# One-hot rows for the slot list of a mixture of experts: on ScalarE instead of VectorE

## Chip, cores and metric

The kernel runs on one core of one Trainium2 chip. Its time is the device time of one execution in microseconds (us); lower is better. The core's engines each run their own list of instructions and meet at semaphores: TensorE (PE in the profile), VectorE (DVE), ScalarE (ACT), GpSimd (POOL) and SyncE (SP), whose list issues most of the DMAs.

## What is computed

Input is `x` of 4 x 1024 tokens with 256 features, all in float32. After a layer norm without weights the result is `x + mamba(xn) + moe(xn)`.

```
mamba:  rn = rmsnorm(xn) * norm_w;  skip = rn @ skip_w.T;  x = silu(conv4(rn @ in_w.T) + conv_b)
        delta = softplus(x @ wd1.T @ wd2.T + wd2_b);  Bm = x @ wB.T;  Cm = x @ wC.T
        h[t] = exp(delta[t] * A) * h[t-1] + delta[t] * x[t] * Bm[t]      (512 channels x 16 states)
        out = xn + ((h . Cm) + x * W_D) * silu(skip) @ out_w.T
moe:    gates = softmax(xn @ Wr)                                          (8 experts)
        inds = the 2 experts with the smallest gates; scores = their gates, normed to sum 1
        out[t] = sum over the 2: score * (silu(xn @ W1[e]) * (xn @ V1[e])) @ W2[e]
```

The mixture is computed sparsely: each token has two (token, expert) pairs, 8192 in all, which are sorted by expert into at most 71 tiles of 128 slots. For that the kernel needs a slot list: for each slot its token and its score.

## The kernel before

**The scan and its units.** The tokens are cut into 16 chunks of 256. A chunk is 32 units: half of the 512 channels (two tiles of 128 partitions) times one of the 16 states. For each unit ScalarE makes `exp(delta * A)` (`exps`, L554, two activations), VectorE makes the product with B (`products`, L1138) and the recurrence (`scan`, L1159, two instructions), GpSimd multiplies two units at once by C (`parts`, L763), and PE adds the result up in PSUM (`sum_parts`, L858) with transposes by the identity. Buffers limit how far the engines can be apart: ScalarE's exps are two units ahead of VectorE in program order, and exps of unit w wait for the scan of unit w - 4. GpSimd is two units behind, PE four.

**The rest of the work** is cut into pieces, and each has a place: behind which unit of its chunk it stands. `pieces(c)` lists them from tables written out by hand (B_PLACES, O_PLACES, F_PLACES), `places_of(engine)` moves some kinds some units later on one engine (table LATER), and every engine runs, unit after unit, its own part of each piece (`do`). Pieces with B or CV, CW, X2, SP, DL prepare the next chunk: chunk input (B1), projection and copy of it to `xin` (B2, ScalarE's L603), convolution (CV, CW, which in chunks 0 and 2 VectorE does from L1283 on, and otherwise ScalarE and GpSimd), Silu (X2, L617), projections to delta, B and C (B3, B4, SP). O pieces finish the chunk before: Silu of the skip branch (O2, L658) and the output products (O1, O3). The kernel has one queue per engine and no other order.

**The router and the slot list.** In chunk 0, R pieces write the normed rows and their logits, and at unit 30 VectorE has run the last router step (`router_slots`), which leaves for each of the 64 columns of pairs `tile` (which slot tile), `lane` (which of 128 rows), `score` and `back`. STAT_END on the semaphore `stat` marks its end; `steps`, a row of 0 to 127 on all partitions, follows it (`ones_set` 2). In chunk 1, eight M pieces (rounds r of 8 columns) stand behind units 2, 4, 6, 8, 12, 18, 21 and 23. In one round VectorE compares `tiles` with `tile` (L1268, 128 x 568) and `steps` with `lane` (L1271, 128 x 1024, one-hot rows into the buffer `hot[r % 2]`), GpSimd multiplies the first result by `back` (L803) and by `score` (L805), and PE, four units later, adds eight matmuls `hot x vals` to bank X (L1004). `placed` counts PE's rounds: from round 2 on VectorE waits for `placed` r - 1 before it writes the buffers again. `hot_set` tells PE that the one-hot rows are there, `val_set` does for the values. Piece MF behind unit 27 reads bank X on VectorE (L1319, L1321, L1323) into `meta` and `idx`; with `idx_set` SP starts the load of W2, which overwrites these buffers, and GpSimd the first two gathers of tokens (L771). From chunk 2 on the expert tiles run as FA, FB and FC pieces, 71 of them up to chunk 14.

ScalarE takes no part in the M pieces: its `do` has no branch for them. Around them its order is, behind unit 33 Silu of O2 (L658), 35 the y copy (L571) and chunk input (L580, L586), 36 the second Silu, 37 the first xin copy (L603), 40 the second, 51 X2 (L617), 54 B3 (L624, L626), 56 B4 (L638, L640) and 59 SP (L647, L650). Unit 32 is the first of chunk 1. All these names of buffers, `hot`, `vals`, `lane`, `steps`, lie in the space of W2, so the profile calls them `w`.

Of the kernel before, what the change touches and what calls it, by code (L numbers as in the profile page):

```python
# [18 lines left out]
ALU = mybir.AluOpType  # L19
ACT = mybir.ActivationFunctionType  # L20
# [199 lines left out]
def mamba_moe(nc, x, norm_w, skip_wT, in_wT, conv_w, conv_b, wd1T, wd2T, wd2_b, wBCT, A_log, W_D, out_wT,  # L220
# [3 lines left out]
    with ctx:  # L224
# [3 lines left out]
        def sem(name):  # L228
            return ctx.enter_context(nc.semaphore(name))
# [126 lines left out]
        res_out = [sem("res_out0"), sem("res_out1")]  # L356
        id_set = sem("id_set")
        added = sem("added")
        hot_set = sem("hot_set")
        val_set = sem("val_set")  # L360
        placed = sem("placed")
# [170 lines left out]
        def _(act):  # L532
# [40 lines left out]
            def do(piece):  # L573
# [31 lines left out]
                elif kind == "CV" and piece[2] not in DVE_CONV:  # L605
                    e, c = piece[1], piece[2]
                    act.wait_ge(conv, KE * c + e)
                    wait_taken(act, "G" if e < 2 else "V", ("B2", e // 2, c))
                    at_least(act, brow_w, 32 * c)
                    nc.scalar.activation(tap[:, 0, :], xin[:, e, 0:CH], ACT.Identity, bias=cb[:, e:e + 1], scale=cw[:, e, 0:1])  # L610
                    for w in range(1, TAPS):
                        ins = nc.scalar.activation(tap[:, w, :], xin[:, e, w:w + CH], ACT.Copy, scale=cw[:, e, w:w + 1])  # L612
                    ins.then_inc(cva, 1)
                elif kind == "X2":
                    c = piece[2]
                    act.wait_ge(conv, KE * (c + 1))
                    nc.scalar.activation(x2[:, c % 2, :, :], x2[:, c % 2, :, :], ACT.Silu).then_inc(x2r, 1)  # L617
                elif kind == "B3":
                    c = piece[2]
                    wait_full(act, "G", piece)  # L620
                    at_least(act, brow_w, 32 * c)
                    if c >= 1:
                        wait_full(act, "V", ("B4", 1, c - 1))
                    nc.scalar.activation(dtT[:, :], bank["G"][:, 0:CH], ACT.Copy)  # L624
                    act.wait_ge(conv, KE * (c + 1))
                    nc.scalar.activation(brow, bank["G"][0:2 * N, CH:2 * CH], ACT.Copy).then_inc(free["G"], 1)  # L626
                elif kind == "B4":
                    q, c = piece[1], piece[2]
                    b = "HV"[q]
                    if c >= 1:  # L630
                        at_least(act, dlt, c)
                    if c >= 2:
                        wait_full(act, "V", ("O3", 1, c - 2))
                        act.wait_ge(uu, 2 * (c - 1))
                    wait_full(act, b, piece)
                    for i in range(2):
                        e = 2 * q + i
                        nc.scalar.activation(y1[:, e, :], bank[b][:, i * CH:(i + 1) * CH], ACT.Abs,  # L638
                                             bias=db[:, e:e + 1]).then_inc(spx, 1)
                        ins = nc.scalar.activation(delta[:, c % 2, e, :], bank[b][:, i * CH:(i + 1) * CH], ACT.Relu,  # L640
                                                   bias=db[:, e:e + 1])
                    ins.then_inc(free[b], 1)
                elif kind == "SP":
                    step, c = piece[1], piece[2]
                    if step == 0:
                        act.wait_ge(spx, 6 * c + 4)
                        nc.scalar.activation(y1[:, :, :], y1[:, :, :], ACT.Exp, scale=-1.0).then_inc(spx, 1)  # L647
                    else:
                        act.wait_ge(spx, 6 * c + 5)
                        nc.scalar.activation(y1[:, :, :], y1[:, :, :], ACT.Ln, bias=1.0).then_inc(spx, 1)  # L650
                elif kind == "O2":
                    q, c = piece[1], piece[2]
                    b = "GV"[q]
                    wait_full(act, b, piece)
                    if c >= 1:
                        wait_full(act, "V", ("O3", 1, c - 1))
                    act.wait_ge(dlt, min(c + 2, CHUNKS))
                    nc.scalar.activation(y1[:, 2 * q:2 * q + 2, :], bank[b][:, :].rearrange("p (k t) -> p k t", k=2),  # L658
                                         ACT.Silu).then_inc(free[b], 1)
                elif kind == "O3":  # L660
                    s, c = piece[1], piece[2]
                    b = "HV"[s]
                    t = SUB * c + s
                    if c < CHUNKS - 1:
                        wait_full(act, b, piece)
                        if c > 0:
                            wait_landed(act, ("O3", 1, c - 1))
                        nc.scalar.activation(mst[:, s, :], bank[b][:, 0:D], ACT.Copy).then_inc(free[b], 1)
                elif kind == "R":
                    i = piece[1]  # L670
                    if i < TT // 2:
                        if i >= 2:
                            wait_full(act, "V", ("R", i - 1))
                            act.wait_ge(xt_out[i % 2], 16 * (i // 2))
                        for t in (2 * i, 2 * i + 1):
                            nc.scalar.activation(tok[:, t % 4, :], xall[:, t, :], ACT.Identity, bias=nmr[:, t:t + 1],
                                                 scale=rstd[:, t:t + 1]).then_inc(xn_r, 1)
                    if 1 <= i <= TT // 2:
                        for k, t in enumerate((2 * i - 2, 2 * i - 1)):
                            wait_full(act, "HV"[k], piece)  # L680
                            at_least(act, lgt, t - 1)
                            nc.scalar.activation(xT[:, k, :, :], bank["HV"[k]][:, 0:D].rearrange("p (k t) -> p k t", k=KD),
                                                 ACT.Copy).then_inc(free["HV"[k]], 1)
                elif kind == "RA":
                    act.wait_ge(stat, STAT_LOGITS)
                    nc.scalar.activation(rt[:, 1], rt[:, 0], ACT.Exp).then_inc(sact, 1)
                elif kind == "FA":
                    j = piece[1]
                    if j < JT:
                        wait_full(act, "H", piece)  # L690
                        if j > 0:
                            wait_taken(act, "V", ("FB", j - 1))
                        nc.scalar.activation(th, bank["H"][:, :], ACT.Tanh, scale=0.5).then_inc(s_th, 1)  # L693
                    if j > 0:
                        wait_full(act, "G", piece)
                        if j > 1:
                            wait_full(act, "X", ("FC", j - 1))
                        nc.scalar.activation(gT, bank["G"][:, :], ACT.Copy).then_inc(free["G"], 1)
                elif kind == "FB":
                    j = piece[1]  # L700
                    if j + 1 < JT:
                        wait_full(act, "X", piece)
                        nc.scalar.activation(xT[:, (j + 1) % 2, :, :], bank["X"][:, 0:D].rearrange("p (k t) -> p k t", k=KD),  # L703
                                             ACT.Copy).then_inc(free["X"], 1)
                elif kind == "FC" and piece[1] > 0:
                    j = piece[1] - 1
                    wait_full(act, "X", piece)
                    if j == 0:
                        act.wait_ge(idx_set, 2)
                        wait_rows(act)  # L710
                    if j >= 2:
                        wait_landed(act, ("FC", j - 1))
                    nc.scalar.activation(tok[:, 2 + j % 2, :], bank["X"][:, 0:D], ACT.Identity,  # L713
                                         scale=meta[:, j:j + 1]).then_inc(free["X"], 1)
# [356 lines left out]
        def _(dve):  # L1071
# [189 lines left out]
            def value_rows(r):  # L1261
# [4 lines left out]
                tiles = csts[:, TT * EXPERTS + TT:TT * EXPERTS + TT + JT].unsqueeze(1).to_broadcast([P, ROUND, JT])  # L1266
                at_least(dve, val_set, 3 * r)
                v.tensor_tensor(vals[r % 2][:, :, JT:2 * JT], tiles, tile[:, at].unsqueeze(2).to_broadcast([P, ROUND, JT]), ALU.is_equal).then_inc(val_set, 1)  # L1268
                if r == 0:
                    dve.wait_ge(ones_set, 2)  # L1270
                v.tensor_tensor(hot[r % 2], steps.unsqueeze(1).to_broadcast([P, ROUND, P]),  # L1271
                                lane[:, at].unsqueeze(2).to_broadcast([P, ROUND, P]), ALU.is_equal).then_inc(hot_set, 1)

            def do(piece):
                kind = piece[0]
# [125 lines left out]
```

## Time and profile before

| | |
|---|---|
| median of 3 runs | 1282.13 us (1279.8 to 1283.07) |
| the profiled execution: its own time | 1284.09 us |
| its span, from the first to the last instruction | 1282.3 us |
| busy: PE, VectorE, ScalarE, GpSimd | 1073.0, 1170.8, 1013.4, 1003.4 us |
| mean granted TensorE clock | 0.926 |
| DMA | 195.08 MB, mean 152 GB/s |

A line of the timeline has the start, the duration, the engine, the line of the kernel, the operation, output and inputs with their shapes (partitions x elements), and in brackets the idle time before it with what ended it. A line merged from several instructions (x2) has their duration from the first start to the last end. The groups of a view by line have the number of instructions, busy us, mean ns of one, and the idle time of the engine before them. Ends of consecutive instructions of VectorE and ScalarE overlap the next start by some tenths of a microsecond.

### The profile page before, as it was taken

The numbers are of one execution on the slowest core, as the hardware profiler recorded it, in microseconds if no ns is written. First come the engines' busy times: TensorE is split into PE (matmuls) and PEld (weight loads), VectorE is DVE, ScalarE is ACT, GpSimd is POOL, SyncE is SP. The second block draws the span as 40 slices with busy tenths as digits, with TensorE's granted clock in tenths as the row PEclk, the third lists the DMA queues.
The fourth block names the chain that finished last, engine by engine and source line by source line (L and its number), as shares of the span: only waits on it lengthen the run. The fifth ranks groups of instructions, "written<-read, shape, count | busy, mean of one in ns | idle before, by whom it ended". The sixth has DMA issues, their size and how long they took to land.

```text
span 1282.3 us, 20051 instructions
## 1 busy us (share of the span) xinstructions
PE 1073.0 (84%) x5406; PEld 807.0 (63%) x5406; DVE 1170.8 (91%) x2145; ACT 1013.4 (79%) x2153; POOL 1003.4 (78%) x602
## 2 busy tenths in 40 slices
PE   3379376587998989999989999898999999998766
PEld 2268265465766666676767666676767667675555
DVE  5874899899999999999989899999989899999896
ACT  2797345589898888879888898889888898988862
POOL 1396277678898979888888988989898988989654
PEclk8686597799999999899999999999999999999987
DMA  7467723745554453545545454555545455545436
GB/s 227 143 205 253 267 77 106 231 139 146 147 146 140 141 160 120 150 141 145 146 133 155 121 154 138 146 157 144 146 123 155 135 145 148 155 122 140 126 125 190
DMA packets 87117, 195.08 MB, mean 152 GB/s; under 512 B 11184, under 2 KB 47152, under 8 KB 86928
## 3 DMA queue, kind: packets, MB, share of 16 engines
q1 hardware_dynamic: 69008, 171.18, 41.4%
q0 software_dynamic: 17712, 22.55, 10.6%
q8 instruction: 47, 0.77, 0.2%
q14 instruction: 62, 0.51, 0.1%
q10 hardware_dynamic: 288, 0.07, 0.0%
HBM read 171.22 MB, written 26.48 MB: 154 GB/s over the span
## 4 chain that ended last, share of the span: by engine, by line
PE 32%; ACT 21%; POOL 17%; issue 13%; DVE 12%; DMA 4%; DVEq 0%; POOLq 0%; ACTq 0%
POOL part L763 11%; ACT aexp L554 8%; PE yps L858 7%; PE bankX L1051 5%; DVE hb L1159 5%; PE bankV L1041 4%; PE bankH L1017 4%; DVE bps L1138 4%; DMA acc<-scr,idx 3%; ACT tap L612 3%; ACT L554 2%; PE bankG L898 1%; POOL scr L771 1%; POOL acc L819 1%; POOL tap L793 1%
## 5 line engine op out<-in xcount | busy, mean ns | idle before, releaser
L763 POOL TENSOR_TENSOR part<-hb,bcr 128x1024 f32<-128x1024 f32 x256 | 625.2, 2449 | 147.1 <-DVE hb L1159 102.5
L1159 DVE TENSOR_TENSOR_SCAN hb<-aexp,carry,bps 128x256 f32<-128x256 f32 x768 | 545.6, 733 | 11.4 <-ACT aexp L554 11.4
L554 ACT ACTIVATE aexp<-delta,Am 128x256 f32<-128x256 f32 x1024 | 446.9, 503 | 54.2 <-DVE hb L1159 52.7
L858 PE MATMUL yps<-idn,part 128*128 128x128 f32 x2048 | 300.2, 287 | 92.8 <-POOL part L763 88.4
L858 PEld LDWEIGHTS yps<-idn,part 128*128 128x128 f32 x2048 | 250.9, 148 | 164.9 <-POOL part L763 97.7
L1138 DVE TENSOR_TENSOR bps<-ups,bcr 128x512 f32<-128x512 f32 x512 | 345.2, 674 | 1.1
L1159 DVE TENSOR_TENSOR_SCAN hb<-aexp,bps 128x256 f32<-128x256 f32 x256 | 167.8, 673 | 23.9 <-ACT aexp L554 23.3
L1051 PE MATMUL bankX<-w,scr 128*128 x568 | 143.2, 397 | 21.8 <-ACT scr L703 19.4
L1017 PE MATMUL bankH<-w,scr 128*128 x284 | 137.9, 608 | 2.1 <-issue 2.1
L1041 PE MATMUL bankV<-v,scr 128*128 x284 | 134.2, 595 | 4.7 <-ACT xin L603 3.3
L1051 PEld LDWEIGHTS bankX<-w,scr 128*128 128x128 f32 x568 | 107.8, 198 | 43.0 <-issue 29.8
L819 POOL DMA_INDIRECT acc<-scr,idx x71 | 114.2, 1609 | 22.4 <-ACT scr L713 7.9
L793 POOL TENSOR_TENSOR tap<-tap 128x512 f32<-128x512 f32 x56 | 78.4, 1400 | 10.3 <-ACT tap L612 10.0
L771 POOL DMA_INDIRECT scr<-xt,idx x71 | 72.3, 1018 | 12.4 <-issue 7.4
L1017 PEld LDWEIGHTS bankH<-w,scr 128*128 128x128 f32 x284 | 51.0, 195 | 42.6 <-issue 40.6
L1041 PEld LDWEIGHTS bankV<-v,scr 128*128 128x128 f32 x284 | 48.4, 190 | 40.3 <-issue 40.3
L612 ACT ACTIVATE tap<-xin,cw 128x256 f32<-128x256 f32 x168 | 72.5, 496 | 0.0
L713 ACT ACTIVATE scr<-bankX,meta 128x256 f32<-128x256 f32 x71 | 33.1, 466 | 49.1 <-PE bankX L1051 49.1
L1327 DVE SCALAR_TENSOR_TENSOR scr<-scr,bankH 128x512 f32<-128x512 f32 x71 | 47.5, 669 | 26.3 <-ACT scr L693 26.2
L693 ACT ACTIVATE scr<-bankH 128x512 f32<-128x512 f32 x71 | 41.9, 590 | 27.8 <-PE bankH L1017 27.8
L554 ACT ACT_TABLE_LOAD x48 | 61.6, 1283 | 0.9
L424 POOL TENSOR_TENSOR delta<-delta,y 128x1024 f32<-128x1024 f32 x15 | 35.3, 2355 | 33.3 <-ACT y L650 33.2
(187 smaller groups left out, 1616.9 us busy)
## 6 DMA issues: line engine op xcount, KB each, us to landing
bcr<-brows SPq DMA_DIRECT2D x256, 512.0 KB
w<-in_W SPq DMA_DIRECT2D x2, 4096.0 KB, 21.9
xch<-in_x SPq DMA_DIRECT2D x16, 256.0 KB, 3.8
w<-in_x SPq DMA_DIRECT2D x4, 1024.0 KB, 9.8
xt<-scr SPq DMA_DIRECT2D x16, 256.0 KB, 2.8
acc<-scr SPq DMA_DIRECT2D x16, 256.0 KB, 2.7
v<-in_V SPq DMA_DIRECT2D x1, 4096.0 KB, 14.9
acc<-mst POOLq DMA_DIRECT2D x15, 256.0 KB
```

What stands on the lines that cost most here:

```text
L554: nc.scalar.activation(aexp[:, w % EXP_SLOTS, i, :], delta[:, c % 2, e, :], ACT.Exp, scale=Am[:, e, n:n + 1]).then_inc(s_a, 1)
L612: ins = nc.scalar.activation(tap[:, w, :], xin[:, e, w:w + CH], ACT.Copy, scale=cw[:, e, w:w + 1])
L763: nc.gpsimd.tensor_tensor(part[:, slot:slot + 2, :, :], hb[:, state:state + 2, :, :], bcr[:, row:row + 2, CH:2 * CH].unsqueeze(2).to_broad ...
L771: nc.gpsimd.indirect_dma_start(out=tok[:, j % 2, :], out_offset=None, in_=xt, in_offset=bass.IndirectOffsetOnAxis(ap=idx[:, j:j + 1], axis ...
L793: nc.gpsimd.tensor_tensor(tap[:, 0:2, :], tap[:, 0:2, :], tap[:, 2:4, :], ALU.add).then_inc(cvs, 1)
L819: nc.gpsimd.indirect_dma_start(out=acc, out_offset=bass.IndirectOffsetOnAxis(ap=idx[:, j:j + 1], axis=0), in_=tok[:, 2 + j % 2, :], in_off ...
L858: mm = pe.matmul(yps[:, s, i * P:(i + 1) * P], part[:, w % (2 * PART_PAIRS), i, s * P:(s + 1) * P], idn[:, :], start=(n == 0 and s == 0 an ...
L1017: mm = pe.matmul(bank["H"][:, :], xT[:, j % 2, k, :], w1[:, bass.ds(col + k * FF, FF)], start=(k == 0), stop=(k == KD - 1))
L1041: mm = pe.matmul(bank["V"][:, :], xT[:, j % 2, k, :], v1[:, bass.ds(columns[j] + k * FF, FF)], start=(k == 0), stop=(k == KD - 1))
L1051: mm = pe.matmul(bank["X"][:, 0:D], gT[:, k * P:(k + 1) * P], w2[:, bass.ds(columns[j] + k * D, D)], start=(k == 0), stop=(k == FF // P - 1))
L1138: v.tensor_tensor(bps[w % 2][:, :, :], ups[:, :, :], bcr[:, w % (2 * ROW_PAIRS), 0:CH].unsqueeze(1).to_broadcast([P, 2, CH]), ALU.mult).th ...
L1159: v.tensor_tensor_scan(hb[:, w % STATE_SLOTS, i, :], aexp[:, w % EXP_SLOTS, i, :], bps[w % 2][:, i, :], first, ALU.mult, ALU.add).then_inc ...
```

## The change

VectorE's comparison of `steps` with `lane`, which wrote the one-hot rows of a round, is gone, with the wait for `ones_set` ahead of it. ScalarE gets a branch for the M pieces, with no entry in LATER, so that it stands behind the same units as VectorE's. In each round it runs eight `Abs` activations, one per column, `|lane - steps|` (128 x 128, scale -1, the column of `lane` as bias), waits on a new semaphore `far_set` for the last of them, and then one `Relu` over all eight (128 x 1024, scale -1, bias 1), which makes 1 of distance 0 and 0 of every other. `hot_set` now comes from ScalarE.

```diff
+        far_set = sem("far_set")
...
+                elif kind == "M":
+                    r = piece[1]
+                    if r == 0:
+                        act.wait_ge(stat, STAT_END)
+                        act.wait_ge(ones_set, 2)
+                    if r >= 2:
+                        act.wait_ge(placed, r - 1)
+                    for k in range(ROUND):
+                        at = r * ROUND + k
+                        ins = nc.scalar.activation(hot[r % 2][:, k, :], steps, ACT.Abs, bias=lane[:, at:at + 1], scale=-1.0)
+                    ins.then_inc(far_set, 1)
+                    act.wait_ge(far_set, r + 1)
+                    nc.scalar.activation(hot[r % 2], hot[r % 2], ACT.Relu, bias=1.0, scale=-1.0).then_inc(hot_set, 1)
...
-                if r == 0:
-                    dve.wait_ge(ones_set, 2)
-                v.tensor_tensor(hot[r % 2], steps.unsqueeze(1).to_broadcast([P, ROUND, P]),
-                                lane[:, at].unsqueeze(2).to_broadcast([P, ROUND, P]), ALU.is_equal).then_inc(hot_set, 1)
```

## Rows read from the trace of the kernel before

**Rows 1.** The page, busy time, share of the span and instructions of each engine
```profile
PE 1073.0 (84%) x5406; PEld 807.0 (63%) x5406; DVE 1170.8 (91%) x2145; ACT 1013.4 (79%) x2153; POOL 1003.4 (78%) x602
```

**Rows 2.** Windows: stretch, its us, busy us of PE, PEld, DVE, ACT, POOL, PEclk, DMA share, GB/s
```profile
160.37:235.14 74.77, 53.98 (x308) 47.77 (x307) 74.34 (x124) 39.92 (x80) 55.48 (x30) 0.85 0.30 93
154.80:169.27 14.47, 11.88 (x62) 10.52 (x63) 14.47 (x23) 13.65 (x24) 11.51 (x6) 0.76 0.34 115
205.83:227.75 21.92, 15.24 (x86) 12.18 (x86) 21.81 (x36) 14.79 (x30) 16.57 (x10) 0.89 0.37 98
```

**Rows 3.** Groups by line, 159 to 236 us: busy, mean ns, idle before
```profile
L803 POOL TENSOR_TENSOR w<-w 128x568 f32<-128x568 f32 x8 | 16.5, 2058 | 14.4 <-DVE w L1268 14.4
...
L1271 DVE TENSOR_TENSOR w<-w 128x1024 f32<-128x1024 f32 x8 | 9.7, 1215 | 0.0
L805 POOL TENSOR_TENSOR w<-w 128x568 f32<-128x568 f32 x8 | 9.1, 1141 | 0.6
```

**Rows 4.** Timeline of VectorE: start, us, line, operation
```profile
161.54 1.21 DVE L1271 TENSOR_TENSOR w<-w 128x1024 f32<-128x1024 f32 x1
162.68 0.14 DVE L1147 TENSOR_REDUCE carry<-hb 128x4 f32<-128x4 f32 x1
...
170.26 1.37 DVE L1159 TENSOR_TENSOR_SCAN hb<-aexp,carry,bps 128x256 f32<-128x256 f32 x2
...
173.97 0.40 DVE L1283 TENSOR_SCALAR x<-xin,cw,cb 128x256 f32<-128x256 f32 x1
...
183.89 0.41 DVE L1283 TENSOR_SCALAR x<-xin,cw,cb 128x256 f32<-128x256 f32 x1
...
226.28 1.21 DVE L1271 TENSOR_TENSOR w<-w 128x1024 f32<-128x1024 f32 x1
...
233.18 0.73 DVE L1159 TENSOR_TENSOR_SCAN hb<-aexp,carry,bps 128x256 f32<-128x256 f32 x1
...
235.14 0.23 DVE L1319 COPY meta<-bankX 128x71 f32<-128x71 f32 x1
```

**Rows 5.** Timeline of GpSimd, first and last round
```profile
161.70 2.06 POOL L803 TENSOR_TENSOR w<-w 128x568 f32<-128x568 f32 x1 [0.68 <-DVE w L1268]
...
229.67 4.68 POOL L763 TENSOR_TENSOR part<-hb,bcr 128x1024 f32<-128x1024 f32 x2
```

**Rows 6.** Timeline of PE, rounds 1, 5 and 7
```profile
174.11 2.11 PE L1004 MATMUL bankX<-w 128*128 128x142 f32 x16
...
219.42 2.11 PE L1004 MATMUL bankX<-w 128*128 128x142 f32 x16
...
233.00 2.11 PE L1004 MATMUL bankX<-w 128*128 128x142 f32 x16
```

**Rows 7.** ScalarE's groups over the whole span, shapes apart
```profile
L554 ACT ACTIVATE aexp<-delta,Am 128x256 f32<-128x256 f32 x1024 | 446.9, 503 | 54.2 <-DVE hb L1159 52.7 <-POOL delta L424 0.7
...
L554 ACT ACT_TABLE_LOAD x48 | 61.6, 1283 | 0.9
...
L693 ACT ACTIVATE scr<-bankH 128x512 f32<-128x512 f32 x71 | 41.9, 590 | 27.8 <-PE bankH L1017 27.8
...
L703 ACT ACTIVATE scr<-bankX 128x256 f32<-128x256 f32 x71 | 26.8, 378 | 9.5 <-PE bankX L1034 9.5
...
L650 ACT ACTIVATE y<-y 128x1024 f32<-128x1024 f32 x16 | 16.9, 1058 | 0.2
```

**Rows 8.** Timeline of ScalarE, six Exp in a row
```profile
271.08 2.49 ACT L554 ACTIVATE aexp<-delta,Am 128x256 f32<-128x256 f32 x6
```

**Rows 9.** Timeline of ScalarE where rounds 0 and 1 will be put
```profile
163.50 0.90 ACT L554 ACTIVATE aexp<-delta,Am 128x256 f32<-128x256 f32 x2
...
168.44 0.20 ACT L600 ACTIVATE xin<-xin 128x12 f32<-128x12 f32 x1
168.67 0.60 ACT L603 ACTIVATE xin<-bankG 128x512 f32<-128x512 f32 x1
```

**Rows 10.** Chain that ended last, in order of time, 154 to 262 us
```profile
237.91 8.58 DMA scr<-xt,idx
```

## The prediction

> **What bounds the kernel now.** I read the page first: VectorE is busy for 91% of the span, GpSimd and ScalarE for 78% and 79% [rows 1]. That average doesn't say what the edit is worth, so the second view is the stretch in which its rounds run, from the first one-hot comparison to the first read of the finished slot list. There VectorE is busy 74.3 of 74.8 us and ScalarE 39.9 [rows 2]: VectorE sets the pace and ScalarE idles nearly half of the time. Third, the groups by line show the eight comparisons (L1271, 9.7 us) and what stands around them [rows 3]. Last comes the timeline of each engine, for the order: ScalarE's idle time is not spread evenly. From 154.80 to 169.27 it is busy 13.65 of 14.47 us [rows 2], and that is where two of the eight rounds will be put.
>
> **What VectorE gives up.** L1271 takes 1.215 us [rows 3], and the next instruction starts 1.14 us after it (161.54 to 162.68 in the first round [rows 4]; the last round's starts at 226.28). Eight times 1.14 is 9.1 us, all in a stretch without idle time. The waits that go with it end earlier anyway.
>
> **What GpSimd gets back.** L803 and L805 have one shape and one operation, yet take 2.06 and 1.14 us [rows 3]. The first L803 runs from 161.70 to 163.76; L1271 ends at 162.75 [rows 4, 5]. So it seems that L803 stands still until L1271 is through, then needs its 1 us. Without L1271 it should take 1.14: GpSimd is 0.92 us earlier in each round. The Trainium skill has the rule in SBUF — State Buffer, section "SBUF: two separate sides": a VectorE instruction with two SBUF inputs and a GpSimd one that reads SBUF take a shared port pair in turn, for the whole instruction, and ScalarE has its own ports. The trace agrees with its first half by the 2.06 against 1.14; with ScalarE as the writer no row shows it.
> That counts once. The read of the slot list (L1319, 235.14) comes right behind VectorE's scan and right behind PE's last round (233.00 and 2.1 long) [rows 4, 6]. In PE's order that round stands behind a sum of the scan's products, the first of the two that GpSimd makes from 229.67 on, right behind L803 and L805 of the last round [rows 5]. GpSimd's side therefore has to move too: the last round yields 0.92, not 1.14. Were L803 to stay at 2.06, the last round would yield nothing and the sum would be 3.4 rather than 4.3 us.
>
> **What ScalarE takes on, per round.** Eight Abs of 128x128 with a bias column, a wait for the last, one Relu of 128x1024. Nothing of this size stands in the trace. The nearest: Exp of 128x256 with a scale column from SBUF, 0.503 us alone, and six of them in 2.49 us, so (2.49 - 0.50) / 5 = 0.40 from start to start [rows 7, 8]. From 256 to 512 columns a copy goes from 0.378 to 0.591 us [rows 7], 0.83 ns a column, so 128 columns fewer take off 0.11: 0.29 from start to start, 0.39 for the last. Relu is as long as Ln of 128x1024, 1.058 [rows 7], of which the next start overlaps 0.1. One round, M: 7 x 0.29 + 0.39 + 0.03 (wait) + 0.95 = 3.4 us. Lower bound: seven starts at 0.23, the spacing of the 12-column copy [rows 9], + 0.30 + 0.95 = 2.9. Upper bound: no overlap, 8 x 0.39 + 0.03 + 1.06 = 4.2. I take 3.4, since every run of like activations in the trace overlaps. Eight rounds are 27 us, against 35 us idle; only their places matter.
>
> **First place: the convolution of chunk 2.** ScalarE's order is exps, Silu, round 0, exps, the y copy, chunk input, exps, Silu, round 1, exps, then the xin copy (L603), which ends at 169.27 with 0.8 us idle since 154.80 [rows 2, 9]. With two rounds ahead of it, it ends at 169.27 + 2 x 3.4 = 176.1. VectorE's L1283 reads it, and starts at 173.97 today [rows 4], at 171.7 without two comparisons. So VectorE stands for 4.4 us there and is 2.1 us later than today (2M - 4.7). The exps that the scans before it need are ready: the tightest pair starts at 163.50 [rows 9], its first half is there at 164.0 + 3.4 = 167.4, and its scan, the second of the pair at 170.26 [rows 4], would come near 168.6.
> **After it** the second xin copy comes 0.8 (exps) + 3.4 + twice 0.8 + 0.6 = 6.4 us behind the first, at 182.5; its reader is at 183.89 today [rows 4] and at 184.8 then (2.1 - 1.14 later), so that it doesn't wait. Rounds 2, 3 and 4 give back 3 x 1.14 = 3.4: 1.3 us ahead of today.
> **Second place: rounds 5 to 7.** Between 205.83 and 227.75 ScalarE works 14.8 us [rows 2]; less 0.5 for the second Exp of the last pair and 0.3 for exps that then overlap their neighbours, 14.0. With three rounds that is 24.2 us from 204.5, so 228.7; the scan at 233.18 [rows 4] would be at 233.18 - 1.3 - 3.4 = 228.5. A wait of 0.2 us. As a formula the scan stands at 205.83 + (2M - 4.7 - 3.4) + 14.0 + 3M - 233.18 = 5M - 21.5 against today: -4.5 us at M = 3.4, and never better than what VectorE's own sum gives.
> **The waits that are added.** far_set is in M, and what is queued behind it, the exps, is paid above. STAT_END and ones_set are set by router steps that VectorE runs ahead of the scan that lets ScalarE go on at 154.80; round 0 comes later than that. The closest wait for placed is that of round 7 for PE's round 5, which ends at 221.5 today [rows 6] and hangs on ScalarE's Silu, 0.7 us earlier then: 220.8, when ScalarE arrives at 220.9. PE waits for hot_set: round 1 is ready ahead of a table load, one pair of exps and the two xin copies, 1.3 + 0.8 + 0.8 us before 176.1, so at 173.2, and PE takes it at 174.11 today [rows 6]. No DMA moves.
>
> **The sum.** +2.1 (first place), -5 x 1.14 = -5.7 (rounds 2 to 6), -0.9 (round 7), +0.2 (second place): -4.3 us. Behind the slot list everything hangs on it: the first gather goes out at 237.91, and its landing 8.6 us later ends the wait of the transposes behind it [rows 10]; that moves as one piece. The profiled execution took 1284.09 us with a span of 1282.3; minus 4.3 it is 1279.8. The median of the runs is 1282.13, 2.0 below the profiled one; minus 4.3 it is **1277.8**.
>
> **Rivals.**
> - **Rounds cost more (M 3.7 to 4.2).** Both places grow: at 4.2, 5 x 4.2 - 21.5 = -0.5, so 1281.6. For it: none of the overlap figures is from 128 columns. Against: the overlaps of [rows 8]. Chance 0.27.
> - **ScalarE covers both places.** It needs M near 2.4, or a xin copy that isn't waited for. Then all of 8 x 1.14 less 0.2 is kept: 1273.2. Against: the lower bound 2.9 gives only -5.5, 1276.6. Chance 0.08.
> - **Slower: ScalarE becomes the bound of the stage.** If a small Abs costs as much as an isolated 256-column Exp, 0.50, with no overlap, M = 8 x 0.50 + 0.03 + 1.06 = 5.1 and 5M - 21.5 = +4.0: 1286.1. It decides from M = 4.3. Against: 12 columns take 0.20 us [rows 9], so size does count. Chance 0.11, with the variant that Abs wants another function table than Exp: two loads of 1.28 us [rows 7] a round, M = 6.0, 1290.6. Against that: the Abs of L638 runs behind Exp, and none of the trace's table loads is on its line.
> The Trainium skill speaks for the slower rival: VectorE: DVE Perf Modes, section "The TRN2 errata", says that the latency of an SBUF source is exposed between instructions, so that many small tiles pay it each time, and advises 512 elements or more. Here each Abs has 128. Taken as full exposure it would be the upper bounds above; no row shows it for 128 columns.
> - **The forecast.** Chance 0.54.
>
> **Range and chances.** A measurement can tell 0.3%, 3.8 us, from no change. The forecast is only 0.5 beyond that, and each 0.1 us of M moves it by up to 0.5. Three quarters of its chance and the full-cover case are faster: 0.48. The rest of it and the dearer rounds are the same: 0.41. Slower: 0.11. The range goes from 1274, close to the full-cover case, past the upper bound of M (1281.6) by most of the scatter of the runs, 3 us, to 1284.
>
> **What would show it.** L1271 gone; ScalarE with 64 Abs near 0.39 and 8 Relu near 1.06 us; L803 at 1.14; a wait of VectorE's L1283 for ScalarE's xin of about 4 us near 172, none like it later; the read of the slot list near 230.8 instead of 235.14. A round of ScalarE at 3.9 us or more, exps that VectorE waits for near 228, or loads before each Abs would prove it wrong. So would a wait moved behind the slot list, if the gather lands no earlier.

## The result, and the profile after

22 runs of each kernel: median 1281.38 us (1277.29 to 1285.93) after the change, 1284.43 us (1279.8 to 1287.6) before. The ratio is 0.9979, with a 95% interval of 0.9969 to 0.9988: faster by 2.7 us of 1284 (the medians lie 3.05 apart), clear of no change, but less than the 0.3% that the prediction took as the least that a measurement can tell. Timed a second time, with 8 runs of after and 17 of before, the ratio was 0.9965 (0.9950 to 0.9980).

First the page's line of busy time. Its columns are those of [rows 1].

```profile
PE 1079.1 (84%) x5406; PEld 810.0 (63%) x5406; DVE 1163.4 (91%) x2137; ACT 1038.8 (81%) x2225; POOL 996.1 (78%) x602
```

VectorE's sum is 7.4 us smaller than in [rows 1], ScalarE's 25.4 larger, GpSimd's 7.3 smaller. Next, the same stretch as in [rows 2], from VectorE's first comparison of a round to the read of the slot list, with the same columns:

```profile
161.84:232.95 71.11, 53.50 (x308) 46.82 (x307) 66.50 (x117) 62.85 (x150) 48.21 (x30) 0.84 0.31 97
```

It is 71.11 us long, where it was 74.77. VectorE is no longer busy all the time: 66.5 of 71.1 us. ScalarE went from 39.9 to 62.9. The groups by line between 159 and 236 us, with the columns of [rows 3]; L694 is the Abs and L697 the Relu, and L817 and L819 are GpSimd's two products (L803 and L805 before):

```profile
L694 ACT ACTIVATE w<-w 128x128 f32<-128x128 f32 x64 | 19.5, 388 | 0.2 <-PE bankX L1018 0.2
...
L817 POOL TENSOR_TENSOR w<-w 128x568 f32<-128x568 f32 x8 | 9.2, 1144 | 18.3 <-DVE w L1282 18.3
L819 POOL TENSOR_TENSOR w<-w 128x568 f32<-128x568 f32 x8 | 9.1, 1142 | 0.6
L697 ACT ACTIVATE w<-w 128x1024 f32<-128x1024 f32 x8 | 8.5, 1058 | 0.3
```

L817 and L819 now cost the same, 1.14 us. The product that took 2.06 in [rows 3] had stood still behind VectorE's comparison. ScalarE's writing of the one-hot rows doesn't hold it up: the first L817 runs from 163.17 to 164.31, beside ScalarE's Relu from 163.68 to 164.74. The timeline of ScalarE, for rounds 0, 1 and 7:

```profile
161.22 2.43 ACT L694 ACTIVATE w<-w 128x128 f32<-128x128 f32 x8
163.68 1.06 ACT L697 ACTIVATE w<-w 128x1024 f32<-128x1024 f32 x1
164.64 0.89 ACT L555 ACTIVATE aexp<-delta,Am 128x256 f32<-128x256 f32 x2
...
171.19 2.43 ACT L694 ACTIVATE w<-w 128x128 f32<-128x128 f32 x8
173.65 1.06 ACT L697 ACTIVATE w<-w 128x1024 f32<-128x1024 f32 x1
174.73 1.28 ACT L555 ACT_TABLE_LOAD   x1
...
177.07 0.60 ACT L604 ACTIVATE xin<-bankG 128x512 f32<-128x512 f32 x1
...
223.17 2.45 ACT L694 ACTIVATE w<-w 128x128 f32<-128x128 f32 x8 [0.21 <-PE bankX L1018]
...
227.41 0.45 ACT L639 ACTIVATE y<-bankH,db 128x256 f32<-128x256 f32 x1
...
230.27 2.53 ACT L555 ACTIVATE aexp<-delta,Am 128x256 f32<-128x256 f32 x6
```

Round 0 runs from 161.22 to the next start at 164.64: 3.42 us. The xin copy (L604, L603 before) starts at 177.07. The timeline of VectorE (L1282 is the comparison that stays, L1293 the first step of a convolution, L1304 the product of O1, L1329 the read of the slot list; they were L1268, L1283, L1294 and L1319):

```profile
161.84 1.25 DVE L1282 TENSOR_TENSOR w<-w 128x568 f32<-128x568 f32 x1
...
166.85 1.60 DVE L1282 TENSOR_TENSOR w<-w 128x568 f32<-128x568 f32 x1
...
173.17 0.69 DVE L1304 TENSOR_TENSOR y<-bankH,y 128x512 f32<-128x512 f32 x1 [0.89 <-PE bankH L888]
174.84 0.69 DVE L1304 TENSOR_TENSOR y<-bankV,y 128x512 f32<-128x512 f32 x1 [0.98 <-PE bankV L888]
177.70 0.41 DVE L1293 TENSOR_SCALAR x<-xin,cw,cb 128x256 f32<-128x256 f32 x1 [2.17 <-ACT xin L604]
...
184.09 1.16 DVE L1293 TENSOR_SCALAR x<-xin,cw,cb 128x256 f32<-128x256 f32 x1
...
210.11 0.94 DVE L1293 TENSOR_SCALAR x<-xin,cw,cb 128x256 f32<-128x256 f32 x1
...
223.44 1.62 DVE L1282 TENSOR_TENSOR w<-w 128x568 f32<-128x568 f32 x1
...
230.95 0.75 DVE L1173 TENSOR_TENSOR_SCAN hb<-aexp,carry,bps 128x256 f32<-128x256 f32 x1
...
232.95 0.23 DVE L1329 COPY meta<-bankX 128x71 f32<-128x71 f32 x1
...
245.63 0.75 DVE L1173 TENSOR_TENSOR_SCAN hb<-aexp,carry,bps 128x256 f32<-128x256 f32 x1 [3.33 <-ACT aexp L555]
```

Three waits in a row stand between 171 and 178 us: 0.89 and 0.98 for PE's results, and 2.17 for the xin copy, 4.0 in all. The first two hang on ScalarE as well. PE stood 2.68 us for ScalarE's chunk input (L581), which round 0 alone delays, and runs the products of O1 (L888) behind it:

```profile
166.65 1.06 PE L900 MATMUL bankG<-idn,xch 128*128 128x128 f32 x4 [2.68 <-ACT xch L581]
```

L1293 starts 15.86 us behind the first comparison, where it was 13.60 in [rows 2, 4]: 2.3 us late. And look at the durations: in rounds 1 and 7 L1282 takes 1.60 and 1.62 us, and 0.74 in rounds 2, 3 and 4. The trace of before has the same in a smaller measure. Its lines of GpSimd and VectorE, for the L1283 that follows round 2 and for the L1268 of round 7:

```profile
179.91 2.35 POOL L763 TENSOR_TENSOR part<-hb,bcr 128x1024 f32<-128x1024 f32 x1
181.48 0.93 DVE L1283 TENSOR_SCALAR x<-xin,cw,cb 128x256 f32<-128x256 f32 x1
...
223.40 2.35 POOL L763 TENSOR_TENSOR part<-hb,bcr 128x1024 f32<-128x1024 f32 x1
224.98 1.38 DVE L1268 TENSOR_TENSOR w<-w 128x568 f32<-128x568 f32 x1
```

And GpSimd's two parts at the same places in after:

```profile
182.74 2.35 POOL L777 TENSOR_TENSOR part<-hb,bcr 128x1024 f32<-128x1024 f32 x1
...
222.09 2.37 POOL L777 TENSOR_TENSOR part<-hb,bcr 128x1024 f32<-128x1024 f32 x1
```

The part of after's round 7 ends at 224.46, and L1282, begun at 223.44, ends 0.60 us later. In before the part ends at 225.75 and L1268 0.61 us later. The L1283 or L1293 of the other pair ends 0.15 us behind its part in both traces. So these two instructions of VectorE stand until GpSimd is through. What changed is where they meet the part. VectorE reaches L1283 1.57 us after the start of the part in before and 1.35 us in after, so that it stands 0.22 us longer. That is what VectorE has gained a round (1.14) less what GpSimd has (0.92).

The stages, in five profiles of the two kernels (two of before, three of after), each from its first comparison: to the read of the slot list, and to the fifth scaling of `ups`, VectorE's first step of chunk 2. The third column is what is left up to the last such scaling of the kernel, the fourth how late the first comparison is in the execution.

| profile | slot list read | chunk 2 | rest | first comparison at |
|---|---|---|---|---|
| before | 74.77 | 89.46 | 986.1 | 160.4 |
| before, again | 74.78 | 88.88 | 987.1 | 160.5 |
| after | 71.11 | 85.44 | 987.4 | 161.8 |
| after, again | 71.01 | 84.77 | 981.4 | 161.1 |
| after, timed | 70.99 | 84.82 | 987.4 | 160.9 |

Up to the slot list the stage repeats to 0.1 us and the change takes 3.7 us out of it. Up to chunk 2 it repeats to 0.7 us, and the lead is 4.2 between the means. What is left of the kernel repeats to 6 us only. So a single profile says much of the stage and nothing of the total.

### The profile page after: what moved, and what is told of

Its sections match the earlier page's. It is cut to its first block, busy times and chain, and to the rows that moved or that the text cites. A ratio compares the mean times of both kernels' runs of the same rounds, so it can differ in the third digit from the quotient of the medians.

```text
span 1281.1 us, 20116 instructions
## 1 busy us (share of the span) xinstructions
PE 1079.1 (84%) x5406; PEld 810.0 (63%) x5406; DVE 1163.4 (91%) x2137; ACT 1038.8 (81%) x2225; POOL 996.1 (78%) x602
## 4 chain that ended last, share of the span: by engine, by line
PE 34%; ACT 26%; POOL 17%; issue 11%; DVE 8%; DMA 3%; DVEq 0%; POOLq 0%; ACTq 0%
POOL part L777 11%; ACT aexp L555 9%; PE yps L872 7%; PE bankX L1065 5%; PE bankH L1031 5%; PE bankV L1055 4%; DVE hb L1173 3%; ACT tap L613 3%; DVE bps L1152 2%; ACT L555 2%; DMA acc<-scr,idx 2%; PE bankG L922 2%; POOL acc L833 2%; POOL tap L807 2%; PE bankG L912 1%
## 5 line engine op out<-in xcount | busy, mean ns | idle before, releaser
L555 ACT ACT_TABLE_LOAD x48 | 61.6, 1283 | 0.9
```

What stands on the lines that cost most here:

```text
L555: nc.scalar.activation(aexp[:, w % EXP_SLOTS, i, :], delta[:, c % 2, e, :], ACT.Exp, scale=Am[:, e, n:n + 1]).then_inc(s_a, 1)
```

## The experiments

**The same two kernels once more.**

> The kernel before, unchanged, for a second profile. Theory A (the stage gains 3.7 to 4.0 us and the rest of the difference is scatter of the start and of the granted TensorE clock): the start of chunk 1 and the granted clock between 250 and 350 us differ from those of the first profile by up to 1.5 us and 0.1, and the slot list is read 74.8 us after VectorE's first comparison, as before. Theory B (the change itself lowers the clock behind the stage): the clock there is 1.00 again.

> The kernel after, unchanged. Theory A: from the first comparison of a round to the read of the slot list 71.1 us again, whatever the start; the granted TensorE clock between 246 and 316 us may be 1.00 this time. Theory B: it is again between 0.80 and 0.94 there, and 1 to 2 us of the stage's gain are gone by 350 us.

Theory A held. The profiles are the second and fourth of the table. From 250 to 320 us the granted clock was 0.91 in the first profile of after and 0.97 in that of before; but the second profile of before has 0.92 there and the second of after 0.94. The rest after chunk 2 was 986.1 and 987.1 in the profiles of before and 987.4 and 981.4 in those of after. The one execution of after took 1275.47 us and that of before 1284.55. Of the 9.1 us between them 4.1 lie between the first comparison and chunk 2 and 5.6 in the rest; the first comparison itself came 0.7 us later in after.

**Rounds 0 and 1 back on VectorE.**

```diff
+DVE_HOT = (0, 1)
...
-                elif kind == "M":
+                elif kind == "M" and piece[1] not in DVE_HOT:
                     r = piece[1]
+                    at_least(act, hot_set, r)
...
+                if r in DVE_HOT:
+                    if r == 0:
+                        dve.wait_ge(ones_set, 2)
+                    v.tensor_tensor(hot[r % 2], steps.unsqueeze(1).to_broadcast([P, ROUND, P]),
+                                    lane[:, at].unsqueeze(2).to_broadcast([P, ROUND, P]), ALU.is_equal).then_inc(hot_set, 1)
```

> Rounds 0 and 1 stay VectorE's comparison, 2 to 7 are ScalarE's. Theory A (VectorE waits 4.0 us for ScalarE's xin copy because two rounds stand ahead of it): no wait there, so that the stage loses nothing at the first place and keeps 5 x 1.14 + 0.9 - 0.6 for the longer waits at the port GpSimd shares = 6.0 us against before (2.3 better than after): read of the slot list 68.8 us behind the first comparison, ratio to before 0.995. Theory C (the gain of the stage is lost behind it, by a limit that doesn't move with the slot list): ratio 0.998 as after, however early the slot list is.

Measured: ratio 0.9979 (0.9966 to 0.9992), slot list at 69.96, chunk 2 at 84.05. The wait for the xin copy is gone, as theory A has it; but of the 6.0 us only 4.8 came. The ratio is that of theory C, and 0.995 lies outside its interval. The profile doesn't bear theory C out up to chunk 2: the stage is 1.0 us shorter than in after there, by the means of the table. All timings are set against their stages behind the last experiment. VectorE's waits in the stage (total us, times, longest) show what took their place:

```profile
DVE hb L1175 <- POOL part L779: 1.3, 1, 1.3
DVE w L1284 <- PE bankX L1020: 1.0, 1, 1.0
```

Before round 7 VectorE now waits for PE's round 5 (`placed`), 1.0 us. PE runs it behind the projections B3, which hang on ScalarE's Silu, which stands behind ScalarE's round 5. That is the wait that the prediction called the closest. The 1.3 us have a releaser that fits badly: the part that ended then isn't the one which that scan needs, and ScalarE's exps for it had started at 229.41, behind round 7 and B4. The scan starts at 230.09, 0.68 us behind them, which is the distance in after too (230.27 and 230.95). So it is ScalarE again. GpSimd's timeline of this kernel holds both forms of the product within one execution:

```profile
163.36 2.06 POOL L819 TENSOR_TENSOR w<-w 128x568 f32<-128x568 f32 x1 [0.69 <-DVE w L1284]
...
178.33 1.14 POOL L819 TENSOR_TENSOR w<-w 128x568 f32<-128x568 f32 x1 [3.11 <-DVE w L1284]
```

In round 0, where VectorE writes the one-hot rows, it takes 2.06 us; in round 2, where ScalarE does, 1.14.

**One more activation in every round.**

```diff
-                    act.wait_ge(far_set, r + 1)
+                    act.wait_ge(far_set, 2 * r + 1)
+                    nc.scalar.activation(hot[r % 2], hot[r % 2], ACT.Abs).then_inc(far_set, 1)
+                    act.wait_ge(far_set, 2 * r + 2)
```

> Each ScalarE round gets one more activation over 128x1024 (an Abs of what is already positive) with its own wait: M = 4.45 instead of 3.42 us. Theory A with the formula 5M - 21.5: the first place adds 2 x 1.03 = 2.1 and the second 3 x 1.03 = 3.1, so that the slot list is read 75.5 to 76 us behind the first comparison, 0.7 to 1 us later than before the change: ratio 1.001. Theory D (ScalarE has idle time enough and only the first place hurts): 2.1 us more than after, ratio 0.9995.

Measured: slot list at 76.14, 5.1 us later than in after, ratio 1.0009 (0.9996 to 1.0021). The formula has 5 x 1.03 = 5.15. VectorE's timeline shows both places (lines two higher than in after):

```profile
174.02 0.69 DVE L1306 TENSOR_TENSOR y<-bankH,y 128x512 f32<-128x512 f32 x1 [2.94 <-PE bankH L890]
175.69 0.69 DVE L1306 TENSOR_TENSOR y<-bankV,y 128x512 f32<-128x512 f32 x1 [0.98 <-PE bankV L890]
178.71 0.41 DVE L1295 TENSOR_SCALAR x<-xin,cw,cb 128x256 f32<-128x256 f32 x1 [2.33 <-ACT xin L604]
...
225.17 1.05 DVE L1284 TENSOR_TENSOR w<-w 128x568 f32<-128x568 f32 x1 [0.48 <-PE bankX L1020]
...
231.18 0.75 DVE L1175 TENSOR_TENSOR_SCAN hb<-aexp,carry,bps 128x256 f32<-128x256 f32 x1 [1.13 <-ACT aexp L555]
...
234.89 0.74 DVE L1175 TENSOR_TENSOR_SCAN hb<-aexp,carry,bps 128x256 f32<-128x256 f32 x1 [1.67 <-ACT aexp L555]
```

The first place holds 2.94 + 0.98 + 2.33 = 6.25 us of waits, 2.2 more than in after; the second, 0.48 + 1.13 + 1.67 = 3.3 us, where after has 0.2 at most. Theory D, which knew only the first place, is out by the slot list. By the ratio alone it would be hardly out, since the interval starts at 0.9996. The formula's offset was 0.6 us too good: it gives +0.75 against before at M = 4.45, and 76.14 is +1.37.

**Rounds 0 and 1 alone on ScalarE.** `DVE_HOT = (2, 3, 4, 5, 6, 7)` in the same edit.

> ScalarE makes rounds 0 and 1 alone, VectorE compares in rounds 2 to 7 as before. Theory A: VectorE waits 4.0 us for the xin copy and has saved 2.3 less 0.5 of longer waits, so the read of the slot list comes 2.2 us later than before the change, 77.0 us behind the first comparison, and the ratio is 1.0017. Rival (the wait is taken from idle time later in the stage): 74.8 and 1.000. The GpSimd product L803 takes 1.14 us in rounds 0 and 1 and 2.06 in the others.

Measured: ratio 1.0015 (1.0002 to 1.0027), the slower side, as expected. Round 7 begins 66.87 us behind round 0, where it was 64.61: 2.3 us late, by waits of 0.9, 1.0 and 2.1 us at the first place. The slot list at 78.5 was 1.5 later than expected, by a wait of 1.5 us for PE's last round, which took 2.75 us there and 2.1 in [rows 6]. The GpSimd product took 1.14 us in two rounds and 2.06 in six (mean 1.828).

**Rounds 0, 1 and 7 on VectorE.** `DVE_HOT = (0, 1, 7)`, and a wait of VectorE for `hot_set` where ScalarE made the round before.

> Rounds 0, 1 and 7 on VectorE, 2 to 6 on ScalarE. With only 0 and 1 there, GpSimd's chain from round 7 on set the slot list. If that is right, the last round on VectorE costs the 0.92 us that GpSimd's product then stands still: slot list 70.9 us behind the first comparison (70.0 with only 0 and 1). If ScalarE's exps set it instead, 69 us or less, since ScalarE has a round less ahead of them.

Measured: slot list at 69.59, chunk 2 at 84.35, ratio 0.9949 (0.9929 to 0.9968). Of the two ways named neither was right. ScalarE's exps had set the list with rounds 0 and 1 there, for 1.3 us, and no scan waits for them now. But VectorE's own comparison takes 1.14 us of that back, VectorE is without a wait from round 7 to the read at 230.76, and PE's last round, behind GpSimd's parts, ends at 230.73. So the gain is 0.4 us and not over 1. By the ratio this version is as good as the best below.

**All rounds on ScalarE, one unit later.**

```diff
-    "ACT": {"B4": 1, "SP": 1, "O2": 1, "B3": 2, "X2": 1, "D": 6, "B2": 1},
+    "ACT": {"M": 1, "B4": 1, "SP": 1, "O2": 1, "B3": 2, "X2": 1, "D": 6, "B2": 1},
```

> All rounds on ScalarE, each one unit later in its order (one entry in the table LATER). Round 1 then stands behind the xin copy, round 5 behind the Silu of X2 and round 7 behind the projections B4. Theory A: VectorE waits for the xin copy for 1.0 to 1.2 us instead of 4.0, PE's round 5 isn't held up by B3 and so neither is round 7; the limit becomes ScalarE's round 7, done 66 us behind the first comparison, and the slot list is read at 68.3 to 68.8: 2.5 us better than after, ratio to before 0.995. Rival (places don't matter, ScalarE's total does): 71.0 as after.

Measured: ratio 0.9959 (0.9946 to 0.9972), slot list at 72.61, chunk 2 at 84.97. The front half went nearly as expected: VectorE has no wait for the xin copy any more, but 1.7 us for PE's products of O1, ahead of which round 0 still stands, and round 7 begins 59.0 us behind round 0, where after has 61.6. The back half did not. ScalarE's round 7 stands behind B4 now, ends at 68.4, and VectorE waits 2.5 us for the exps behind it. Then PE's last round, whose operands came late, ran slow. The timeline of PE, rounds 6 and 7 (L1018), and the windows before and during round 7 (the columns of [rows 2]; PEclk is the third number from the end):

```profile
221.18 2.11 PE L1018 MATMUL bankX<-w 128*128 128x142 f32 x16
225.60 1.14 PE L872 MATMUL yps<-idn,part 128*128 128x128 f32 x8 [2.32 <-POOL part L777]
228.60 4.16 PE L1018 MATMUL bankX<-w 128*128 128x142 f32 x16 [1.85 <-ACT w L697]
```

```profile
222.00:228.60 6.60, 2.43 (x20) 1.94 (x18) 4.56 (x10) 6.57 (x19) 5.79 (x4) 0.84 0.36 132
228.60:232.80 4.20, 4.20 (x18) 4.20 (x19) 1.99 (x4) 4.18 (x8) 1.66 (x1) 0.50 0.34 125
```

Sixteen matmuls took 4.16 us at a granted clock of 0.50, the lower level of 1.2 GHz; the sixteen of round 6 took 2.11. PE had been busy for 2.43 of the 6.6 us ahead of the slow ones. The slot list was read 4 us later than expected, but the start of chunk 2 is level with after, since the conversion into `idx` that follows the read took 0.28 us and not 2.0 (see the end).

**One unit later, rounds 0 and 7 on VectorE.** Both edits. Round 0 has nothing to hide behind, round 7 is off ScalarE's queue at its end.

> ScalarE's rounds one unit later as before this, and rounds 0 and 7 on VectorE. No wait for the xin copy, none for PE's round 5. Theory A: six times 1.14 less 0.5 of port waits: slot list at 68.4 us, ratio 0.995. If GpSimd's port wait in round 7 weighs as in the kernel before, it is no better than with all rounds on ScalarE.

> ScalarE one unit later and rounds 0 and 7 on VectorE, again. From the stage alone it should be 1.6 to 2.3 us ahead of after, so 0.9955 to 0.996 of the kernel before; 0.9934 in its first timing had to be partly chance. A ratio below 0.995 again would mean that it gains something behind the stage.

Measured: 0.9934 (0.9916 to 0.9952) and 0.9951 (0.9933 to 0.9968), chunk 2 at 83.12 and 82.74, 1.9 to 2.3 us ahead of after. It is the fastest of all versions up to chunk 2, with 6.1 to 6.4 us against the mean of before, 0.5% of the time, and medians of 1278.06 and 1277.29 us. The total does not tell it from after: on the chip on which both were timed the ratios are 0.9951 and 0.9965, with intervals that overlap. The second expectation said that below 0.995 would mean a gain behind the stage; 0.9951 gives no such sign. The slot list at 70.2 is 1.8 later than expected: VectorE waits 1.6 and 1.7 us for PE's last round, slow as above (3.70 and 3.77 us). Here it isn't late by ScalarE: PE stood 3.23 us for GpSimd's part ahead of it. That cost little, since the conversion behind the read takes 0.35 us in VectorE's timeline and not 2.0. It has the read, the conversion into `idx` and the next wait for ScalarE.

```profile
232.08 0.23 DVE L1338 COPY meta<-bankX 128x71 f32<-128x71 f32 x1 [1.67 <-PE bankX L1020]
...
232.55 0.35 DVE L1342 CAST idx<-w 128x71 int32<-128x71 f32 x1
...
242.99 0.75 DVE L1175 TENSOR_TENSOR_SCAN hb<-aexp,carry,bps 128x256 f32<-128x256 f32 x1 [3.20 <-ACT aexp L556]
```

> As the run before, with round 1 on VectorE too. Round 1 then costs VectorE 1.14 us that ScalarE, which stands behind the xin copy at that place, would have hidden: 84.3 us from the first comparison to the start of chunk 2, ratio 0.9960 to 0.9965.

Measured: slot list at 71.26, chunk 2 at 84.14 and ratio 0.9962 (0.9950 to 0.9973), the last two as expected. The slot list comes 1.1 us later than with round 1 on ScalarE, which is the comparison's 1.14: one unit later, round 1 costs the stage nothing on ScalarE.

**After, timed again.**

> The kernel after, unchanged, timed on the chip on which the next run is timed. Theory A: 0.997 to 0.998 of the kernel before, as in its first timing; first half of chunk 1 to the start of chunk 2 (first comparison to the fifth scaling of ups) 84.8 to 85.4 us, and the time behind it between 981 and 988 us at random.

Measured: 0.9965 (0.9950 to 0.9980), chunk 2 at 84.82, rest 987.4. The interval overlaps that of the first timing and holds the 4.2 us of the stage (0.9968), which the first one, 0.9969 to 0.9988, just misses.

**All timings against their stages.** The lead of a version's chunk 2 over the mean of before (89.17), divided by 1284, gives the ratio that the version should have if nothing changes behind the stage. Each timed ratio is against runs of before that were taken with it.

| version | slot list read | chunk 2 | ratio from the stage | ratio timed |
|---|---|---|---|---|
| after | 71.04 (mean of 3) | 85.01 (mean of 3) | 0.9968 | 0.9969 to 0.9988 |
| after, timed | as above | as above | 0.9968 | 0.9950 to 0.9980 |
| rounds 0 and 1 on VectorE | 69.96 | 84.05 | 0.9960 | 0.9966 to 0.9992 |
| one more activation a round | 76.14 | 90.03 | 1.0007 | 0.9996 to 1.0021 |
| rounds 0 and 1 alone on ScalarE | 78.5 | 91.26 | 1.0016 | 1.0002 to 1.0027 |
| rounds 0, 1 and 7 on VectorE | 69.59 | 84.35 | 0.9962 | 0.9929 to 0.9968 |
| one unit later | 72.61 | 84.97 | 0.9967 | 0.9946 to 0.9972 |
| one unit later, 0 and 7 on VectorE | 70.16 | 83.12 | 0.9953 | 0.9916 to 0.9952 |
| the same, timed again | 70.19 | 82.74 | 0.9950 | 0.9933 to 0.9968 |
| one unit later, 0, 1 and 7 on VectorE | 71.26 | 84.14 | 0.9961 | 0.9950 to 0.9973 |

Seven of ten intervals hold the ratio from the stage. Three miss it, two from above and one from below. So the stage accounts for the time of the versions as a whole; for the three that miss, what makes the difference isn't known.

## Why the prediction was right or wrong

- **What VectorE gives up: right.** 1.14 us a round: from 6.14 to 5.01 us between rounds 0 and 1.
- **What GpSimd gets back: the size right, the consequence only half drawn.** 1.14 for 2.06 us in all eight rounds. What follows from 0.92 being less than 1.14 was counted for round 7 alone (see the sum).
- **M: right.** 3.42 us against 3.4, from Abs of 0.388 (0.39) and Relu of 1.058.
- **First place: right, the parts shifted.** 4.0 us of waits against 4.4, 2.3 us late against 2.1. Half of it showed as a wait for PE, whose O1 hangs on the same ScalarE queue by way of the chunk input. The text had only the path by the xin copy. Since that one ends last (177.67), the other changed nothing in the sum.
- **Second place: right.** A wait of 0.2 us for exps in the second profile of after, and 5M in `longer_round`.
- **placed: right that it was closest.** ScalarE waited 0.21 us for it in after, and VectorE 1.0 as soon as rounds 0 and 1 were taken back.
- **The sum: 0.5 to 0.6 us too good at the slot list.** 4.3 was forecast, 3.7 to 3.8 came (74.77 against 71.11, 71.01 and 70.99). By terms: +2.3 at the first place for +2.1; -5.3 to -5.4 from there to round 7 for "-5 x 1.14 = -5.7 (rounds 2 to 6)"; and -0.65 from round 7 on for -0.9 + 0.2. The step that failed is the term of rounds 2 to 6, which took each comparison off at its full 1.14. GpSimd moves up by 0.92 only, so VectorE meets GpSimd's part 0.22 us sooner and stands for it that much longer: L1293 behind round 2 took 1.16 us in the three profiles of after (1.15 in one) for 0.93 and 0.92 in before. The text charged this difference in round 7 alone ("the last round yields 0.92, not 1.14"), for another reason, the order of PE's work behind GpSimd's parts. There the size came out, and L1282 took 1.62 us for 1.38. The next L1293 took 0.94, 0.84 and 0.80 for 0.79, so its share isn't steady. Another 0.22 in round 1 lies before the xin wait and costs nothing.
- **Behind the slot list: moved as one piece, roughly.** By chunk 2 the lead was 4.2 us, 0.5 more than at the list. The gather explains most of that: from its issue to PE's transposes it took 8.7 and 8.1 us in before and 8.3, 7.7 and 7.9 in after. With that scatter the 0.5 can't be put down to the change.
- **The number 1277.8.** The measured median is 1281.38, 3.6 us more. 2.3 of these are the base: the median of before was 1282.13 in the 3 runs that the forecast started from, and 1284.43 in 22. The rest is the change, 4.3 forecast against 3.05 between the medians. That 1281.38 lies inside the stated range is luck: the room was left for dearer rounds (1281.6), and the rounds weren't dearer.
- **The other step that failed: how much of the sum a timing shows.** The text put 4.3 us against a bound of 3.8 and gave "faster by over 0.3%" the larger chance. The margin of 0.5 was no more than the error of the sum, and less than what the rest of the kernel does by itself: its 986 us differ by 6 us between executions of one kernel. The first timing says 0.21%, within the bound, the second 0.35%. What the 1.5 us between the first timing and the stage's 4.2 are isn't settled. Chance is enough for it. The first comparison also came later in after, at 160.9 to 161.8 us in three profiles, than in before, at 160.4 and 160.5. But `scalar_one_later` (160.2) and `longer_round` (160.7), with as much and more on ScalarE, start as early as before.
- **Rivals.** Dearer rounds: not at this M, but right in kind, as `longer_round` shows. Full cover: no. ScalarE as the bound: on a line through after with the slope of 5, the point of no gain is at M = 4.2 rather than 4.3 (71.04 + 5 x (M - 3.42) = 74.77), an estimate. No table load was added for Abs: ScalarE goes from Silu at 171.19 and from Exp at 161.22 right into it. By the Trainium skill (VectorE: DVE Perf Modes, section "The TRN2 errata") small tiles with SBUF sources pay a latency each. Measured, one Abs of 128 columns takes 0.388 us, and 0.29 from start to start, of which by the slope of 0.83 ns a column 0.11 are the columns. So the fixed part is most of it, but not the upper bound of the prediction, since neighbours overlap.

## What to carry to other kernels

Before work is moved to an engine that idles on average, walk its queue at the places where the new work will stand: two of eight rounds stood ahead of a copy for which VectorE waits, and caused 4.0 us of waits, nearly what four rounds save (4 x 1.14). Then try the entry in the order table together with leaving single pieces where they were. One unit later alone gave nothing more by chunk 2 (84.97 against 84.8 to 85.4); with rounds 0 and 7 left on VectorE it gave 1.9 to 2.3 us more than the plain move. Leaving rounds 0 and 7 on VectorE without the entry was not run. And where a forecast lies within 0.5 us of what a timing can tell, judge it by a stage that repeats to 0.1 us, not by the total.

## What was not expected of the hardware

- GpSimd and VectorE hold each other up in both directions. Removing VectorE's comparison took 0.92 us off GpSimd's product in each of eight rounds, and 0.22 us came back on each of three VectorE instructions that stand for a GpSimd part (L1282 of rounds 1 and 7, L1293 behind round 2). The Trainium skill, in the section that the prediction cites (SBUF — State Buffer, "SBUF: two separate sides"), says of the shared port pair that whichever of the two "starts first gets the pair for the whole instruction" and the other blocks. The traces agree, by these durations. The prediction reckoned with GpSimd's standing only. VectorE's scans and products with B, which have one operand in PSUM, don't stand: in the stage they take 0.66 to 0.75 us while a part runs.
- The conversion of 128x71 to int32 that ends the slot list took 2.0 us in before and after, 2.0 to 2.1 in three other versions, and 0.28 to 0.55 in the versions where GpSimd's part is nearly through when it starts. It ends 0.04 to 0.06 us behind that part in all thirteen profiles. Before has, for example:

```profile
235.22 2.34 POOL L763 TENSOR_TENSOR part<-hb,bcr 128x1024 f32<-128x1024 f32 x1 [0.87 <-DVE hb L1159]
235.61 2.01 DVE L1323 CAST idx<-w 128x71 int32<-128x71 f32 x1
```

  So it seems to stand for GpSimd too, and up to 1.7 us of a late slot list cost nothing.
- A slow round of PE costs time where the round is the last. Sixteen matmuls of 142 columns took 2.11 us at a granted clock of 1.00, which is 2.4 GHz, 4.16 at 0.50, which is 1.2 GHz, and between the two where the clock changed within the round (3.70 at 0.54). That is nothing special to the later placements: before has it in four of its eight rounds, two of them shown here, but not in the last.

```profile
183.22 3.32 PE L1004 MATMUL bankX<-w 128*128 128x142 f32 x16
...
226.79 3.72 PE L1004 MATMUL bankX<-w 128*128 128x142 f32 x16
```

  In the versions with one unit more the last round is slow, after PE had stood for its operands (1.85 us) or for GpSimd's part (3.23 us) shortly before. It lasted 4.16, 3.70, 3.77 and 3.03 us, which took 0.9 to 2 us back at the slot list. A pause doesn't settle it alone: PE was busy for 3.39 of the 6.6 us ahead of round 3 in after and in `longer_round`, and that round took 3.22 us in the one and 2.11 in the other.
